# A graph network's edge attributes split in wider, earlier rounds, and one PSUM bias row written by two engines in turn

## What is computed

```python
h = relu(layernorm(x))
x = x + gin_layer(h)                     # two 512<->1024 products with batch norms
h = relu(layernorm(x))
# layer 1, per edge:
m = mish(mish(concat(h[src], h[dst], edge_attr) @ W1 + b1) @ W2 + b2)
agg = segment_sum(m, dst)
y = h + mish(concat(h, agg) @ W3 + b3) @ W4 + b4
x = x + layernorm(y) * gamma + beta
mish(z) = z * tanh(softplus(z))
```

## Time and profile before

| what | value |
|---|---|
| median of 3 runs | 1154.87 us (1153.55 to 1155.7) |
| the profiled execution, its own time | 1156.01 us |
| its span, first to last instruction | 1154.1 us |
| busy: PE / DVE / ACT / POOL | 1042.5 / 876.5 / 896.4 / 729.3 us |
| mean granted TensorE clock | 0.963 of full speed |
| all 79 steps of the edge loop | about 420 to 1070 us |

### The profile page before, as it was taken

One profiled execution on the slowest core, in us unless ns is written; L12 is line 12 of the kernel. 1 busy time (PEld: TensorE's weight loads), 2 busy tenths in 40 slices (PEclk: granted clock), 3 DMA queues, 4 the chain that ended last, 5 costly groups with the idle time before them and its releaser, 6 DMA issues. The chain is left out here.

```text
span 1154.1 us, 18647 instructions
## 1 busy us (share of the span) xinstructions
PE 1042.5 (90%) x5603; PEld 865.5 (75%) x5604; DVE 876.5 (76%) x1504; ACT 896.4 (78%) x1119; POOL 729.3 (63%) x638
## 2 busy tenths in 40 slices
PE   3558999995079999999999999999999999999997
PEld 1126899994068988888888888888888888888796
DVE  7898345624032538988999999999999899889786
ACT  6986736523031269999999999999999999999584
POOL 6874353523344548777778888888878777770217
PEclk8879999998589999999999999999999999999999
DMA  2006624464436538766666666676676666662002
GB/s 101 8 1 149 108 82 110 107 205 107 111 119 218 116 84 180 149 154 142 142 137 136 142 137 140 139 140 142 135 146 134 142 142 135 144 135 50 1 1 90
DMA packets 79792, 137.42 MB, mean 119 GB/s; under 512 B 11067, under 2 KB 36924, under 8 KB 79622
## 3 DMA queue, kind: packets, MB, share of 16 engines
q0 software_dynamic: 38048, 87.58, 37.9%
q1 hardware_dynamic: 41702, 49.32, 13.9%
HBM read 113.33 MB, written 18.29 MB: 114 GB/s over the span
## 5 line engine op out<-in xcount | busy, mean ns | idle before, releaser
L750 POOL DMA_INDIRECT gather_pq<-q_table,dst x157 | 302.6, 1928 | 57.4 <-issue 47.5
L742 POOL DMA_INDIRECT gather_pq<-p_table,src x157 | 188.8, 1203 | 105.8 <-PE banks L1102 52.4
L1118 PE MATMUL banks<-w_lo,h_hi 128*128 128x512 f32 x620 | 244.2, 394 | 2.6 <-DVE banks L2121 1.9
L1119 PE MATMUL banks<-w_hi,h_hi 128*128 128x512 f32 x620 | 242.3, 391 | 0.0
L1123 PE MATMUL banks<-w_hi,h_lo 128*128 128x512 f32 x620 | 166.0, 390 | 0.0
L1118 PEld LDWEIGHTS banks<-w_lo,h_hi 128*128 128x128 f32 x620 | 116.4, 188 | 33.9 <-issue 6.8
L2092 DVE SCALAR_TENSOR_TENSOR h_full<-mish_work,banks 128x512 f32<-128x512 f32 (+1 forms) x154 | 98.4, 680 | 48.7 <-ACT mish_work L1428 47.0
L1123 PEld LDWEIGHTS banks<-w_hi,h_lo 128*128 128x128 f32 x620 | 116.4, 188 | 24.6
L1119 PEld LDWEIGHTS banks<-w_hi,h_hi 128*128 128x128 f32 x620 | 116.5, 188 | 21.2
L2117 DVE SCALAR_TENSOR_TENSOR message<-mish_work,banks 128x1024 f32<-128x1024 f32 x78 | 95.3, 1222 | 8.5 <-ACT mish_work L1452 0.6
L1095 PE MATMUL banks<-ident,gather_pq 128*128 128x128 f32 x628 | 97.6, 277 | 1.8 <-DMA gather_pq<-q_table,dst 0.5
(11 more groups left out here) (272 smaller groups left out, 2665.8 us busy)
## 6 DMA issues: line engine op xcount, KB each, us to landing
edge_attr_parts<-attr_parts SPq DMA_DIRECT2D x79, 128.0 KB, 2.9
edge_attr<-in_edge_attr_t SPq DMA_DIRECT2D x40, 128.0 KB, 2.1
attr_parts<-edge_attr_hi SPq DMA_DIRECT2D x80, 64.0 KB, 1.9
attr_parts<-edge_attr_lo SPq DMA_DIRECT2D x80, 64.0 KB, 1.9
x_nodes<-h_hi POOLq DMA_DIRECT2D x10, 256.0 KB, 13.1
x_nodes<-h_lo POOLq DMA_DIRECT2D x10, 256.0 KB, 7.8
p_table<-p_stage SPq DMA_DIRECT2D x10, 256.0 KB, 2.0
q_table<-agg_nodes SPq DMA_DIRECT2D x10, 256.0 KB, 3.7
```

Of the source, the lines that this page charges most:

```text
L742: nc.gpsimd.indirect_dma_start(GP[:, 2 * j + k, :], None, p_tab[:, :], bass.IndirectOffsetOnAxis(ap=SRC[:, 2 * s + k:2 * s + k + 1], axis= ...
L750: nc.gpsimd.indirect_dma_start(GP[:, 2 * j + k, :], None, q_tab[:, :], bass.IndirectOffsetOnAxis(ap=DST[:, 2 * s + k:2 * s + k + 1], axis= ...
L1118: pe.matmul(at, h_high(s, j)[:, c, e], W2_LO[:, c, :], start=False, stop=False, skip_group_check=True)
L1119: pe.matmul(at, h_high(s, j)[:, c, e], W2_HI[:, c, :], start=False, stop=False, skip_group_check=True)
```

## The change

Attributes: 20 steps (`ATTR_STEPS`) take the place of the 40 rounds. A step loads four pairs in one transfer of 256 KB (`AT_RAW` is twice as large), POOL makes two high and two low tiles in the order high, high, low, low, and SP stores each in one transfer of 128 KB, high parts into a table `attr_high`, low parts into `attr_low`. The first six steps (`ATTR_FIRST`) are done earlier: by POOL between the issue of its additions into X and its wait for them and for `w02`; by SP between the load of `w01` and the wait before the load of `w02`. The load of W1 stands behind step 14 (`ATTR_SECOND`). In the edge loop the attributes of a pair are loaded by two transfers of 64 KB, and the waits count 32.

Bias: in odd steps DVE fills both tiles with one copy of 128 x 1024 (the row is read twice by broadcast), and ACT none for that pair. For the even pairs DVE fills the first and ACT the second, as before (ACT does that in odd steps, for pair s-1). PE's second tile of an odd pair waits for DVE's count.

```diff
@@ -94,7 +94,7 @@
 SLOTS = 4
-ATTR_BREAK = 20
+ATTR_STEPS, ATTR_FIRST, ATTR_SECOND = PAIRS // 4, 6, 14
 BLOCKS = 4
@@ -189,8 +189,8 @@
         XWORK = (XWORK_0[:, :, :], XWORK_1[:, :, :])
-        AT_RAW, _ = sb("edge_attr", [P, 2, PW])
-        B2_ROW, _ = sb("b2_row", [P, 1, DIM], at=place[0] - 4 * 2 * PW)
+        AT_RAW, _ = sb("edge_attr", [P, 2, 2, PW])
+        B2_ROW, _ = sb("b2_row", [P, 1, DIM], at=place[0] - 4 * 4 * PW)
         AT_HI, _ = sb("edge_attr_hi", [P, 2, PW], F32R)
@@ -365,7 +365,7 @@
         q_tab = nc.dram_tensor("q_table", [NP, DIM], F32)
-        at_tab = nc.dram_tensor("attr_parts", [PAIRS, P, PW], F32)
+        at_tabs = [nc.dram_tensor(f"attr_{n}", [PAIRS, EDGE_DIM, PW], F32) for n in ("high", "low")]
         r_tab = nc.dram_tensor("range_table", [GROUPS, R_WORDS], I32)
@@ -403,8 +403,8 @@
         q_moved, p_stored, q_stored = sem("q_moved"), sem("p_stored"), sem("q_stored")
-        attr_raw = [sem(f"attr_raw{j}") for j in range(2)]
-        attr_stored = [sem(f"attr_stored{j}") for j in range(2)]
+        attr_raw = [sem(f"attr_raw_in{j}") for j in range(2)]
+        attr_stored = [[sem(f"attr_{n}_stored{j}") for j in range(2)] for n in ("high", "low")]
         attr_in = [sem(f"attr_in{j}") for j in range(SLOTS)]
@@ -498,39 +498,47 @@
+            def two_pairs(table, n, count):
+                return table[bass.ds(2 * n, 2 * count), :, :].rearrange("(q o) p e -> (o p) q e", o=2)
+            def load_raw(m, j):
+                sp.dma_start(AT_RAW[:, j, :, :], two_pairs(edge_attr_t, 2 * m, 2)).then_inc(attr_raw[j], 16)
+            def store_parts(n, j):
+                for made, part, table, stored in ((attr_hi, AT_HI, at_tabs[0], attr_stored[0]), (attr_lo, AT_LO, at_tabs[1], attr_stored[1])):
+                    sp.wait_ge(made, n + 1)
+                    sp.dma_start(two_pairs(table, n, 1), part[:, j:j + 1, :].bitcast(F32)).then_inc(stored[j], 16)
+            def split_step(m, j, more=True):
+                for k in range(2):
+                    store_parts(2 * m + k, k)
+                if more:
+                    load_raw(m + 2, j)
+            def split_steps(first, end):
+                with sp.Fori(first // 2, end // 2) as i:
+                    for j in range(2):
+                        split_step(2 * i + j, j)
             sp.wait_ge(counts_added, HALVES * GROUPS)
...
                 sp.dma_start(WA0[:, c, :], w01[c * P:(c + 1) * P, :]).then_inc(w01_in, 16)
+            for j in range(2):
+                load_raw(j, j)
+            split_steps(0, ATTR_FIRST)
             sp.wait_ge(z0_part, 2 * NT)
...
-            def load_raw(n, j):
-                sp.dma_start(AT_RAW[:, j, :], edge_attr_t[bass.ds(2 * n, 2), :, :].rearrange("o p e -> (o p) e")).then_inc(attr_raw[j], 16)
-            def store_parts(n, j):
-                for done, part, rows in ((attr_hi, AT_HI, slice(0, EDGE_DIM)), (attr_lo, AT_LO, slice(EDGE_DIM, P))):
-                    sp.wait_ge(done, n + 1)
-                    for k in range(2):
-                        sp.dma_start(at_tab[bass.ds(2 * n + k, 1), rows, :].rearrange("o p e -> (o p) e"),
-                                     part[EDGE_DIM * k:EDGE_DIM * (k + 1), j, :].bitcast(F32)).then_inc(attr_stored[j], 16)
-            def split_pairs(first, end):
-                with sp.Fori(first // 2, end // 2) as i:
-                    for j in range(2):
-                        store_parts(2 * i + j, j)
-                        load_raw(2 * i + 2 + j, j)
-            for j in range(2):
-                load_raw(j, j)
-            split_pairs(0, ATTR_BREAK)
+            split_steps(ATTR_FIRST, ATTR_SECOND)
             sp.wait_ge(mm_done, MM_2)
...
             sp.dma_start(WA[:, :, :], w1[0:2 * DIM, :].rearrange("(k p) n -> p k n", p=P)).then_inc(w1_in, 16)
-            split_pairs(ATTR_BREAK, PAIRS // 2 - 2)
+            split_steps(ATTR_SECOND, ATTR_STEPS - 2)
             for j in range(2):
-                store_parts(PAIRS // 2 - 2 + j, j)
+                split_step(ATTR_STEPS - 2 + j, j, more=False)
             sp.dma_start(B2_ROW[:, :, :], rows[ROW_B2:ROW_B2 + 1, :].partition_broadcast(P)).then_inc(b2_in, 16)
@@ -542,11 +550,14 @@
             sp.wait_ge(p_stored, TABLE_STORED)
-            for j in range(2):
-                sp.wait_ge(attr_stored[j], 16 * PAIRS)
+            for stored in attr_stored:
+                for j in range(2):
+                    sp.wait_ge(stored[j], 16 * ATTR_STEPS)
             def attributes(s, j):
-                sp.dma_start(AT_R[:, j, :].bitcast(F32), at_tab[bass.ds(s, 1), :, :].rearrange("o p e -> (o p) e")).then_inc(attr_in[j], 16)
+                for rows, table in ((slice(0, EDGE_DIM), at_tabs[0]), (slice(EDGE_DIM, P), at_tabs[1])):
+                    sp.dma_start(AT_R[rows, j, :].bitcast(F32),
+                                 table[bass.ds(s, 1), :, :].rearrange("o p e -> (o p) e")).then_inc(attr_in[j], 16)
@@ -694,6 +705,22 @@
+            def attr_parts(first, end):
+                for m in range(first, end):
+                    pool.wait_ge(attr_raw[m % 2], 16 * (m // 2 + 1))
+                    for k in range(2):
+                        if m > 0:
+                            pool.wait_ge(attr_stored[0][k], 16 * m)
+                            pool.wait_ge(attr_lo, 2 * m + k - 1)
+                        nc.gpsimd.tensor_copy(AT_HI[:, k, :], AT_RAW[:, m % 2, k, :]).then_inc(attr_hi, 1)
+                    for k in range(2):
+                        pool.wait_ge(attr_hi, 2 * m + k + 1)
+                        if m > 0:
+                            pool.wait_ge(attr_stored[1][k], 16 * m)
+                        nc.gpsimd.tensor_tensor(AT_LO[:, k, :], AT_RAW[:, m % 2, k, :], AT_HI[:, k, :].bitcast(F32),
+                                                ALU.subtract).then_inc(attr_lo, 1)
             pool.wait_ge(counts_added, HALVES * GROUPS)
@@ -702,6 +729,7 @@
                     nc.gpsimd.dma_start(X[:, nt, :], part[:, nt, :].bitcast(F32), accum_op=ALU.add).then_inc(x_added, 16)
+            attr_parts(0, ATTR_FIRST)
             pool.wait_ge(x_added, 32 * NT)
@@ -712,19 +740,7 @@
-            def attr_parts(n):
-                j = n % 2
-                pool.wait_ge(attr_raw[j], 16 * (n // 2 + 1))
-                if n >= 2:
-                    pool.wait_ge(attr_stored[j], 64 * (n // 2))
-                nc.gpsimd.tensor_copy(AT_HI[:, j, :], AT_RAW[:, j, :]).then_inc(attr_hi, 1)
-                pool.wait_ge(attr_hi, n + 1)
-                nc.gpsimd.tensor_tensor(AT_LO[:, j, :], AT_RAW[:, j, :], AT_HI[:, j, :].bitcast(F32), ALU.subtract).then_inc(attr_lo, 1)
-            for n in range(PAIRS // 2):
-                attr_parts(n)
+            attr_parts(ATTR_FIRST, ATTR_STEPS)
             pool.wait_ge(bn_ready, KH + KD)
@@ -1110,8 +1126,10 @@
                     pe.wait_ge(h_hi, s + 1)
-                if after(s, 2):
-                    pe.wait_ge((b2_first, b2_second)[k], s - 1)
+                if after(s, 2) and k == 1 and j == 0:
+                    pe.wait_ge(b2_second, s)
+                elif after(s, 2):
+                    pe.wait_ge(b2_first, s - 1)
                 else:
@@ -1176,15 +1194,15 @@
                         s = Z1_BEHIND.index(n)
-                        z1(s, s, 64, 16)
+                        z1(s, s, 64, 32)
             z2(0, 0, 0)
             for s in range(2, SLOTS):
-                edge_step(s, s, 64, 16, None)
+                edge_step(s, s, 64, 32, None)
             with pe.Fori(1, EDGE_PAIRS // SLOTS) as i:
                 for j in range(SLOTS):
-                    edge_step(SLOTS * i + j, j, 64 * (i + 1), 16 * (i + 1), 2 * i + (j - 4) // 2)
+                    edge_step(SLOTS * i + j, j, 64 * (i + 1), 32 * (i + 1), 2 * i + (j - 4) // 2)
             for s in range(EDGE_PAIRS - EDGE_PAIRS % SLOTS, EDGE_PAIRS + 4):
-                edge_step(s, s % SLOTS, 64 * (s // SLOTS) + 32 * tiles(s), 16 * (s // SLOTS + 1), (s - 4) // 2)
+                edge_step(s, s % SLOTS, 64 * (s // SLOTS) + 32 * tiles(s), 32 * (s // SLOTS + 1), (s - 4) // 2)
@@ -1452,7 +1470,7 @@
             def b2_second_tile(s, j):
-                nc.scalar.copy(Z2[:, 2 * j + 1, :], B2_ROW[:, 0, :]).then_inc(b2_second, 1)
+                nc.scalar.copy(Z2[:, 2 * j + 1, :], B2_ROW[:, 0, :]).then_inc(b2_second, 2)
@@ -1466,7 +1484,7 @@
                     sq2(s - 2)
-                if after(s, 3) and live(s - 1) and tiles(s - 1) == 2:
+                if j == 1 and after(s, 3) and live(s - 1) and tiles(s - 1) == 2:
                     b2_second_tile(s - 1, 1 - j)
@@ -2117,8 +2135,10 @@
             def b2_first_tile(s, j):
                 dve.wait_ge(msg_full, s - 1)
-                nc.vector.tensor_copy(Z2[:, 2 * j, :], B2_ROW[:, 0, :]).then_inc(b2_first, 1)
+                n = 2 if j == 1 else 1
+                nc.vector.tensor_copy(Z2[:, 2 * j:2 * j + n, :], B2_ROW[:, :, :].broadcast_to([P, n, DIM])).then_inc(b2_first, 1)
 
```

## The result

The changed kernel takes 1111.12 us (median of 4 runs, 1109.59 to 1112.53), the one before, run beside it, 1155.28. The ratio is 0.962, 95% interval 0.960 to 0.964. That is 44.2 us less, where the prediction had 55.7. It lies inside the whole range of 1089 to 1113, but above the 1095 to 1104 that the forecast itself had. The profiled execution has a span of 1110.7 us, 43.4 less than before.

What follows compares the result with a forecast made beforehand. Bounds: PE's 48.8 us wait for POOL's `w1_lo`, and ACT's pace in the edge loop, PE and DVE close behind. Gains 48.8 + 2.1 + 4.8 = 55.7 led from 1154.9 to 1099.2; forecast's own range 1095 to 1104, whole range 1089 to 1113.

Steps and rivals of the forecast that it cites:

- The stall goes whole, 48.8: Ahead of P: PE's wait for POOL's `w1_lo` goes entirely, 48.8 us gained.
- its after-effect, 2.1: Start of P: the granted clock, 0.57 of full in the first 5.00 us behind the wait, becomes full; 2.1 us gained.
- Steps of 4.0 us: POOL's attribute work: a new step of four pairs takes 4.0 us, where two old rounds take 7.3.
- My 0.67 for the issue of a store: SP in the attribute steps: issuing one transfer costs about 0.67 us, part of the chain that sets a step.
- Six early steps in 24 us: POOL's idle time from 128.2: six attribute steps end at 152, and the split of `w02` at 176 instead of 172.1.
- Nothing is late next: P and after: nothing else holds PE up once its wait for `w1_lo` goes, so what follows moves up whole.
- The wide copy takes 1.22: DVE in odd steps of the edge loop: the bias copy of 1024 columns takes 1.22 us, 0.54 more than the narrow.
- ACT's pace without the copy, 16.57: Edge loop: ACT, without its bias copy in even steps, takes 16.57 us for two steps, 0.37 less.
- the path around four steps: Edge loop, through DVE, PE and ACT: 33.28 us, or 16.64 for two steps; 17.05 beside the W3 pieces.
- 4.8 gained in the loop: Edge loop: pairs of steps without W3 pieces gain 6.6 us, those with them lose 1.8, net 4.8 gained.
- DVE becomes the bound in the whole loop: Rival, edge loop: two steps take 17.05 to 17.3, loop 4 to 14 us longer, time 1108 to 1118; chance 0.15.
- The signs: Expected in the trace: `w1_lo` right behind `bn_shift`, attributes done at 235 to 255, exponentials alternating early, no DVE gap 610 to 880.

Runs made afterwards that it cites:

- attributes alone: The attribute part of the change without its bias part, both bias copies as in the kernel before: 1105.68 us against 1154.74, ratio 0.9575.
- bias alone: The bias part of the change on the old attribute rounds of the kernel before: 1159.80 us, ratio 1.0042.
- the kernel whose sums don't wait: The whole change, but in even steps DVE's additions into the node sums take the bias row and don't wait for PE: 1103.44 us, ratio 0.9556.
- two copies and W3 in even steps only: The whole change, but DVE fills odd pairs by two copies, the second behind h_lo, and POOL splits W3 only in even steps: 1093.68 us, ratio 0.9470.

## Why the prediction was right and wrong

- *The stall goes whole, 48.8, and its after-effect, 2.1:* right. The granted clock of the first 5 us of P, 277.8 to 282.8, is 1.00 after (0.57 in the earlier trace rows), and the stage of P and Q ends 2.1 earlier against its start than before. Of the 50.9, attributes alone brought 49.1.
- *Steps of 4.0 us:* 3.45. My 0.67 for the issue of a store was wrong; SP issues most of them in 0.33 to 0.41. The landing was right: the page after has 1.9 and 1.8 us for the 128 KB stores (I took 1.9 to 2.1):

```profile
attr_high<-edge_attr_hi SPq DMA_DIRECT2D x40, 128.0 KB, 1.9
attr_low<-edge_attr_lo SPq DMA_DIRECT2D x40, 128.0 KB, 1.8
```

  The Trainium skill's 2.3 for this size (DMA: Bandwidth & Descriptors, Anatomy of one DMA) is above both; what it gives was measured on transfers that GpSimd issues, and these are SyncE's. Here it didn't matter: POOL had 25 us to spare.
- *Six early steps in 24 us:* 28.9, since the first two ran beside the additions into X. `w02` was issued at 158.5 and its split done at 183.9 (predicted 176), still 24 ahead of the product that needs it (207.58). That POOL ended at 245.1, as predicted (247), is in part two errors that cancel: the late steps began 8 later and took 9 less.
- *Nothing is late next:* nearly. PE was ready for P 2.8 later than before (276.11 + 1.87 against 275.20). 1.5 of it was there before any changed work (below), 0.6 arose by the end of the batch norm, and 0.7 is an effect of the change itself: POOL's low split of W1 now runs beside the layer norm, and one small DVE instruction has to wait for it (VectorE, after):

```profile
273.25 0.84 DVE L1610 SCALAR_TENSOR_TENSOR ln_bias<-ln_mean_var,rstd 128x2 f32<-128x2 f32 x1
```

  It took 0.16 before, and 0.19 with bias alone, and PE waited 0.76 for the scaled nodes.
- *The wide copy takes 1.22:* right, exactly.
- *ACT's pace without the copy, 16.57:* right; 16.56 where nothing else binds.
- *The step that failed: the path around four steps as the longest one, 16.64, hence 4.8 gained in the loop.* The loop lost 4.0, the bias part alone 5.1. Where W3 isn't split, the path itself was sized well (33.28 against 33.50, once the ring was cut). Beside the pieces it was not the longest: the ring took 17.18, and with it cut another ring of two steps stood at 17.13. What I left out is that DVE's additions wait for PE's segment product. This closes a shorter ring of 16.94, in which the wide copy counts once in two steps, not once in four. I had read the odd step as starting "late, behind the node sums", and did not ask what the sums wait for. In the trace of before they show no wait worth the name, as the ring was 0.5 below ACT's pace.
- *The rival "DVE becomes the bound in the whole loop"* had the right time (1108 to 1118) by another mechanism: DVE's total did not bind the change. The measured time fell into the stated range through this rival; the forecast's own 1095 to 1104 missed it.
- *The signs:* in the attribute part they came. In the loop two failed: ACT's exponentials do not alternate near 8.1 and 8.5 after the first few steps (8.48 and 8.47 with a wait for PE), and DVE has gaps beside the W3 pieces (0.42 ahead of its additions). Neither of the two conditions under which the forecast was to fail was met, late steps above 5.6 or a wide copy away from 1.22, and the term of the loop failed all the same: neither of them asks about the path.

## What to carry to other kernels

Before work is added to an engine in a loop, list for each instruction behind it every semaphore it waits on, also those that show no wait now, and add up each closed ring over one, two and four steps; the added time counts in every ring that it lies on, once a turn. An operation whose result is needed a step later belongs behind the ones that others wait for: splitting one copy into two made DVE's work longer and the kernel 13 us faster. And where two engines get in each other's way, place the meeting in the step that has slack: the same splits in other steps gave 4.5 us.

## What the hardware showed that I had not expected

DVE's casts of 1024 columns take 0.69 alone. Beside POOL's low split of 128x128, one of them takes 0.93 or 0.94 in each pair of steps of the change, and 1.21 or 1.22 in the kernel whose sums don't wait. Its subtractions (1.22) grow to 1.31, and to 1.48 where both splits stand in the even step. The Trainium skill (VectorE: DVE Perf Modes, What auto-detection actually checks; SBUF — State Buffer, SBUF: two separate sides) has a mode for operations with one source and SBUF at both ends that takes the port pair shared with POOL. The traces agree: the casts are of that kind and cost half a subtraction; the bias copy, which writes PSUM, takes 0.69 for 512 columns and 1.22 for 1024, so it has no such rate. Two things go beyond it. With two copies and W3 in even steps only, one bias copy in each pair of steps took 0.84 or 0.85, with no split of POOL beside it but a gather (VectorE and GpSimd):

```profile
614.84 0.84 DVE L2139 COPY banks<-b_row 128x512 f32<-128x512 f32 x1
...
614.02 1.02 POOL L758 DMA_INDIRECT gather_pq<-p_table,src  x1
```

The other copies beside gathers, in this kernel and the others, took 0.69, so what lengthened these isn't shown. And a small instruction can stand through several of POOL's in a row, as the 7.28 us of the experiment with attributes alone show, not only through one.

The counting stage ahead of all changed work isn't the same in every execution. Windows of 50 to 98 us (busy PE, PEld, DVE, ACT, POOL, granted clock, DMA share, GB/s), before and then after:

```profile
50.00:98.00 48.00, 30.48 (x117) 13.65 (x116) 45.05 (x133) 33.36 (x65) 33.02 (x55) 0.84 0.02 5
```

```profile
50.00:98.00 48.00, 34.36 (x116) 14.21 (x114) 44.68 (x130) 32.65 (x64) 31.77 (x54) 0.70 0.02 5
```

The granted clock was 0.70 instead of 0.84, and POOL's additions into X were issued 1.5 us later (98.64 against 97.17). In other kernels with the same code there the clock was 0.64 to 0.82 and the additions were issued between 94.85 and 97.98, the lowest clock at 95.81; so the clock alone doesn't set that time, and what does stays open. A difference of a microsecond or two between two single profiles is therefore no finding; the medians are.
